# Moving the experts' down biases and the shared bias into one product per 128 tokens of the mixing stage

## The reference, cut to what matters

```python
x = x + attention(xn) + moe(xn)

# moe, over T = 4096 tokens, E = 8 experts, the best TOPK = 2 of them per token
scores = softmax(xt @ gate_w.T + gate_b)
top_w, top_i = top_k(scores, 2)
gate_dense = sum(one_hot(top_i, 8) * top_w[..., None], axis=1)        # (T, 8), two entries non-zero
def expert(w1e, b1e, w3e, b3e, w2e, b2e):
    h = silu(xt @ w1e.T + b1e) * (xt @ w3e.T + b3e)
    return h @ w2e.T + b2e                                            # b2e: the down bias
y = einsum('etd,te->td', outs, gate_dense)
z = silu(xt @ ws1.T + bs1) * (xt @ ws3.T + bs3) @ ws2.T + bs2         # bs2: the shared bias
moe = y + z
```

## Time and profile before

| what | value |
|---|---|
| time, median of 3 runs (lowest, highest) | 512.99 us (512.96, 513.41) |
| the profiled execution: its own time, its span | 512.58 us, 510.9 us |
| busy share of the span: PE, DVE, POOL, ACT | 88%, 75%, 52%, 46% |
| stages of the profiled execution, by PE | route to 97 us; experts 101 to 296.8; mixing 296.8 to 510.9 |
| TensorE clock granted, mean | 0.936 of full |
| DMA | 78.3 MB, 153 GB/s over the span |

### The profile page before, as it was taken

The page is one execution under the profiler, slowest core; times in us unless marked ns, Lnnn a source line. Parts: engine busy times, 40 slices in busy tenths (PEclk is TensorE's granted clock), DMA queues, the critical chain, the costliest instruction groups (busy, mean ns, idle before and its releaser), DMA issues.

```text
span 510.9 us, 8428 instructions
## 1 busy us (share of the span) xinstructions
PE 448.7 (88%) x2553; PEld 372.1 (73%) x2553; DVE 384.8 (75%) x704; ACT 232.8 (46%) x377; POOL 267.5 (52%) x227
## 2 busy tenths in 40 slices
PE   0768309489999999999999996999999999999997
PEld 0323105268988889888898974888888988898887
DVE  7677899535786777867775566999697969796964
ACT  1537335237668576685766563232323233233231
POOL 4402480374537548475482558886837464737200
PEclk9979755579999999999999998899999999999999
DMA  6999991134644443344444486252625252524111
GB/s 208 359 344 296 320 253 35 42 104 120 192 159 148 138 145 125 118 154 144 138 125 126 139 302 222 83 166 102 186 83 175 94 175 92 171 96 127 41 42 41
DMA packets 46662, 78.32 MB, mean 153 GB/s; under 512 B 6184, under 2 KB 32552, under 8 KB 46624
## 3 DMA queue, kind: packets, MB, share of 16 engines
q1 hardware_dynamic: 37808, 55.90, 31.6%
q0 software_dynamic: 8816, 21.93, 17.1%
HBM read 49.58 MB, written 28.21 MB: 152 GB/s over the span
## 4 chain that ended last, share of the span: by engine, by line
PE 68%; DVE 13%; DMA 7%; issue 7%; ACT 2%; POOL 1%; SPq 1%; DVEq 0%; POOLq 0%; ACTq 0%
PE ps_g L974 20%; PE ps_y L974 9%; PE ps_w L1389 5%; PE ps_w L1391 5%; PE ps_w L1390 5%; PE ps_x L968 3%; PE ps_h L992 3%; DMA xn_rows<-xn 3%; PE ps_w L1451 2%; PE ps_w L1453 2%; PE ps_w L1452 2%; PE ps_T L588 2%; DVE sa L1537 2%; PE ps_y L1001 2%; DVE part_a L1545 1%
## 5 line engine op out<-in xcount | busy, mean ns | idle before, releaser
L911 POOL DMA_INDIRECT xg<-xn_rows,tile_tok x71 | 69.9, 984 | 46.8 <-DVE tile_tok L783 18.8
L1359 POOL DMA_INDIRECT yg<-expert_rows,rows x64 | 70.0, 1093 | 23.9 <-issue 18.2
L1119 DVE TENSOR_TENSOR hid<-ps_g,act 128x512 f32<-128x512 f32 (+1 forms) x36 | 24.2, 672 | 48.7 <-ACT act L1043 48.3
L974 PE MATMUL ps_g<-w_hi,x_hi 128*128 x142 | 57.1, 402 | 0.4 <-issue 0.4
L974 PE MATMUL ps_g<-w_hi,x_lo 128*128 x142 | 56.8, 400 | 0.0
L974 PE MATMUL ps_g<-w_lo,x_hi 128*128 x142 | 56.5, 398 | 0.0
L1389 PE MATMUL ps_w<-col_hi,s_hi 128*128 128x512 f32 x128 | 50.7, 396 | 0.9 <-DVE res L1585 0.8
L1391 PE MATMUL ps_w<-col_hi,s_lo 128*128 128x512 f32 x128 | 50.2, 392 | 0.0
L1390 PE MATMUL ps_w<-col_lo,s_hi 128*128 128x512 f32 x128 | 50.2, 392 | 0.0
L1492 ACT ACTIVATE sact<-ps_w,vec_b 128x512 f32<-128x512 f32 x32 | 22.0, 688 | 58.7 <-PE ps_w L1391 58.7
L974 PE MATMUL ps_y<-w_hi,h_hi 128*128 x142 | 42.9, 302 | 0.5 <-DVE h_lo L1126 0.5
(11 more groups left out here) (210 smaller groups left out, 1292.8 us busy)
## 6 DMA issues: line engine op xcount, KB each, us to landing
expert_rows<-y SPq DMA_DIRECT2D x35, 256.0 KB, 2.2
table<-mix_tables SPq DMA_DIRECT2D x8, 768.0 KB, 7.5
xin<-x SPq DMA_DIRECT2D x16, 256.0 KB, 4.9
xn_rows<-xn SPq DMA_DIRECT2D x16, 256.0 KB, 5.7
xn_columns<-xT SPq DMA_DIRECT2D x8, 512.0 KB, 5.4
col<-xn_columns SPq DMA_DIRECT2D x8, 512.0 KB, 6.3
res<-x SPq DMA_DIRECT2D x16, 256.0 KB, 3.5
out<-res SPq DMA_DIRECT2D x16, 256.0 KB, 2.6
```

Source lines behind the costliest of these rows:

```text
L911: pool.indirect_dma_start(out=xg[b][:, t, :], out_offset=None, in_=xn_d[:, :], in_offset=bass.IndirectOffsetOnAxis(ap=tile_tok[:, 2 * a + ...
L974: mm = nc.tensor.matmul(out, x[:, k, :], w[:, ds(e, 1), k, cols].rearrange("p o n -> p (o n)"), start=(k == 0 and n == 0), stop=(last and ...
L1119: nc.vector.tensor_tensor(hid[:, 0:n, :], ps_g[a % 2][:, 0:n, FF:2 * FF], act1[:, 0:n, :], ALU.mult).then_inc(c_h, 1)
L1359: pool.indirect_dma_start(out=yg[a.buf(2)][:, k, q, :], out_offset=None, in_=y_d[:, :], in_offset=bass.IndirectOffsetOnAxis(ap=picked[a.bu ...
```

## The change

The down bias and the shared bias are no longer added where they arise. For each block of 512 tokens a 128 x 128 matrix `gT[:, i, :]` holds, for each of its four 128-token sub-tiles q, 32 rows (`TERMS`): the dense gates' high halves (8), their low rests (8), the high halves again (8), two rows of ones, and six of zeros. `rows_b[:, q, :]` holds beside them, in the partitions 32q to 32q+31, the down biases' high halves twice, their low halves, the shared bias's low and high half, and zero in all other partitions. One product of the two, 128 x 128 by 256 columns, opens each sub-tile's sum in `outputs`.

- In `route`, `ones2`, `bias_hl`, its zero fills, its split and its DMAs go. POOL makes the dense gates and their halves with five small operations behind its last indirect DMA, in `terms`.
- In `run_experts`, the 71 bias products go. Ahead of the first duo PE turns `terms` with 8 transposes into `ps_y`, ACT copies them to `gT` (2 copies). `b_all`, now 26 rows of b2 three times and bs2 twice, is loaded by 4 DMAs at duo 8 into `rows` (zeroed by POOL at duo 6); ACT makes the high halves at duo 14, POOL three operations at duo 16 that put high and low halves in place, by a mask from five tiny DVE operations at duo 8.
- In `mix`, POOL's `bias(a)` is replaced with `pick(a)`, a 128 x 128 copy of the step's `gT` into `g_now`, and four products are added per `outputs`. DVE's `experts(a, 0)` waits for the DMAs of `res` itself.

```diff
@@ route
-            nc.gpsimd.memset(pick2[:], 0.0).then_inc(s_two, 1)
-            pool.wait_ge(s_two, 1)
-            nc.gpsimd.memset(pick2[0:2, :], 1.0).then_inc(s_two, 1)
+            nc.gpsimd.memset(terms[:], 0.0).then_inc(s_terms, 1)
+            pool.wait_ge(s_terms, 1)
+            nc.gpsimd.memset(terms[:, :, 3 * E:3 * E + 2], 1.0).then_inc(s_terms, 1)
...
+            pool.wait_ge(s_mask, 3)
+            nc.gpsimd.tensor_tensor(dense[:], score, mask[:].rearrange("p e j -> p j e"), ALU.mult
+                                    ).then_inc(s_terms, 1)
+            pool.wait_ge(s_terms, 3)
+            nc.gpsimd.tensor_copy(dense_hi[:], dense[:]).then_inc(s_terms, 1)
+            pool.wait_ge(s_terms, 4)
+            nc.gpsimd.tensor_tensor(terms[:, :, E:2 * E], dense[:], dense_hi[:].bitcast(F32), ALU.subtract)
+            for n in (0, 2):
+                ins = nc.gpsimd.tensor_copy(terms[:, :, n * E:(n + 1) * E], dense_hi[:].bitcast(F32))
+            ins.then_inc(s_terms, 1)
...
-                nc.scalar.activation(bias_hl[:, a.i, :].bitcast(F32), ident[:, 0:1].broadcast_to([P, C]),
-                                     ACT.Copy, scale=0.0).then_inc(s_bzero, 1)
...
@@ run_experts
+                if a == A_ROWS:
+                    sp.wait_ge(c_zero, 1)
+                    for q in range(Q):
+                        sp.dma_start(rows[TERMS * q:TERMS * q + 3 * E + 2, q, :], b_all).then_inc(c_rows, 16)
...
+            def low_rows():
+                pool.wait_ge(c_rhi, 1)
+                pool.wait_ge(c_mask, 4)
+                nc.gpsimd.tensor_scalar(rows[:], rows[:], is_lo[:, 1:2], None, ALU.mult)
+                nc.gpsimd.tensor_scalar(rows_hi[:], rows_hi[:].bitcast(F32), is_lo[:, 2:3], None, ALU.mult
+                                        ).then_inc(c_own, 1)
+                pool.wait_ge(c_own, 1)
+                nc.gpsimd.tensor_tensor(rows_b[:], rows[:], rows_hi[:].bitcast(F32), ALU.add).then_inc(c_rowsb, 1)
...
             def down(a, es):
                 pe.wait_ge(c_hlo, a + 1)
+                if a < 2:
+                    pe.wait_ge(c_gT, a + 1)
                 at_least(pe, c_yc, a - 1)
                 for t in range(tiles(a)):
-                    three(ps_y[a % 2][:, t, :], h_hi[a % 2][:, t], h_lo[a % 2][:, t], es[t],
-                          slice(2 * FF, WALL), False)
-                    mm = nc.tensor.matmul(ps_y[a % 2][:, t, :], ones2[:],
-                                          bias_hl[:, ds(es[t], 1), :].rearrange("p o n -> p (o n)"),
-                                          start=False, stop=True)
+                    mm = three(ps_y[a % 2][:, t, :], h_hi[a % 2][:, t], h_lo[a % 2][:, t], es[t],
+                               slice(2 * FF, WALL), True)
                 mm.then_inc(c_y, 1)
...
-            pe.wait_ge(s_bias, 32)
+            pe.wait_ge(s_terms, 5)
+            for i in range(NSTEP):
+                mm = nc.tensor.transpose(ps_y[i // 4][:].rearrange("p t c -> p (t c)")[:, i % 4 * P:(i % 4 + 1) * P],
+                                         terms[:, i * Q:(i + 1) * Q, :].rearrange("p q n -> p (q n)"), ident[:])
...
@@ mix
-            def bias(a):
-                pool.wait_ge(b_res[a.buf(2)], (a.uses(2) + 1) * 32)
-                nc.gpsimd.tensor_tensor(res[a.buf(2)][:], res[a.buf(2)][:],
-                                        row_b2[:, None, :].broadcast_to([P, Q, C]), ALU.add).then_inc(b_xb, 1)
+            def pick(a):
+                at_least(pool, b_o, a.i * Q - Q)
+                nc.gpsimd.tensor_copy(g_now[a.buf(2)][:], gT[:, ds(a.i, 1), :].rearrange("p o n -> p (o n)")
+                                      ).then_inc(b_gc, 1)
...
                 def mixed(q):
+                    nc.tensor.matmul(ps_w[q][:, 0:C], g_now[a.buf(2)][:], rows_b[:, q, :],
+                                     start=True, stop=False)
                     for k in range(KC):
                         three_rows(ps_w[q][:, 0:C], a_hi, a_lo, k, slice(q * P, (q + 1) * P), o_hi, o_lo,
-                                   k == 0, False)
+                                   False, False)
...
                 if g == 0:
-                    dve.wait_ge(b_xb, a.i + 1)
+                    dve.wait_ge(b_res[buf], (a.uses(2) + 1) * 32)
                     dve.wait_ge(b_gath[buf], (a.uses(2) + 1) * 16 * TOPK * Q)
```

More of the change, by code:

```diff
@@ L54 @@
 EPS = 1e-5
+TERMS = 32
 PIECE = 256
@@ L218, in _, with route @@
                 mix_vector(dve)
-def route(nc, kept, x, first, decay, vec_tf, vec_td, gate_w, gate_b, w_all, w_first, nw_d, b_all, xn_d, xT_d, ident, slots, gates,
-          tile_tok, tile_exp, w_hi, w_lo, bias_hl, ones2):
+def route(nc, kept, x, first, decay, vec_tf, vec_td, gate_w, gate_b, w_all, w_first, nw_d, xn_d, xT_d, ident, slots, gates,
+          tile_tok, tile_exp, w_hi, w_lo, terms):
     with ExitStack() as ctx:
@@ L801, in sem @@
             return kept.enter_context(nc.semaphore(name))
-        s_tok, s_xout, s_bias = placed
+        s_tok, s_xout, s_terms = placed
         raw_vr, col0 = vr[0], col[0]
+        rows, rows_hi, gT, rows_b = bias
+        row32 = sb("row32", [P, 1], I32)
+        is_lo = sb("is_lo", [P, 3], F32)
         NG = 4
@@ L947, in gpsimd @@
                     gather(a + AHEAD)
+                if a == A_ZERO:
+                    nc.gpsimd.memset(rows[:], 0.0).then_inc(c_zero, 1)
+                    nc.gpsimd.iota(row32[:], pattern=[[0, 1]], base=0, channel_multiplier=1).then_inc(c_iota, 1)
+                if a == A_LO:
+                    low_rows()
                 if r == 1 and v == NPIECE:
@@ L1078, in scalar @@
             act.wait_ge(s_tok, 1)
+            for h in range(2):
+                act.wait_ge(c_turn, h + 1)
+                nc.scalar.activation(gT[:, 4 * h:4 * h + 4, :].rearrange("p j n -> p (j n)"),
+                                     ps_y[h][:].rearrange("p t c -> p (t c)"), ACT.Copy).then_inc(c_gT, 1)
             halves(0)
@@ L1094, in scalar @@
                     halves(v)
+                if a == A_HI:
+                    act.wait_ge(c_rows, 16 * Q)
+                    act.wait_ge(c_zero, 1)
+                    nc.scalar.activation(rows_hi[:], rows[:], ACT.Copy).then_inc(c_rhi, 1)
                 if a == DUOS - 4:
@@ L1240, in mix @@
         sa = sb("sa", [P, KC * B, TIMES + 1], F32)
+        g_now = [sb(f"g_now{b}", [P, P], F32R) for b in range(2)]
         table = [sb(f"table{b}", [P, 3, KC, TIMES], F32) for b in range(2)]
```

95 lines of the change are left out of this document (50 added, 45 removed).

## The result

| | before | after |
|---|---|---|
| time, median (lowest, highest; runs) | 512.98 us (512.75, 513.41; 4) | 504.82 us (503.35, 506.79; 4) |
| profiled execution: time, span | 512.58, 510.9 us | 504.14, 502.3 us |
| TensorE clock granted, mean | 0.936 | 0.939 |

By the medians the kernel is faster by 8.2 us. The ratio of the runs is 0.9851, which is 7.6 us, with a 95% interval of 0.983 to 0.9873 (6.5 to 8.7 us). The prediction said 504.3 us and a range of 501.0 to 508.5. The runs of after spread more (3.4 us) than those of before (0.7 us).

What follows compares the result with a forecast made beforehand. PE was taken to bound the expert and mixing stages. The terms, -8.2 + 3.8 - 2.9 - 2.8 + 1.6 - 0.2 = -8.7 us, led from the median of 512.99 to 504.3 us, range 501.0 to 508.5.

Steps and rivals of the forecast that it cites:

- Removed products: Expert stage: 71 bias products go at 0.12 us each, three of them giving nothing; -8.2 us.
- POOL gets 6 us more ... behind 193 us of PE, 0: Expert stage: POOL's added memset, scalings and addition fit beside 80 us free and cost 0.
- Added products: Mixing stage, bound by PE: 32 products at 0.12 us each at the full clock; +3.8 us.
- The stall ahead of values(1): PE's 4.57 us idle shrinks to some 2.5, the clock probably kept; -2.9 us (bounds -1.2 and -3.5).
- The late starts: Mixing steps: most of PE's six late starts, waiting for DVE, end; -2.8 us (bounds -1.7 and -3.1).
- POOL's five in the route: Route: POOL's five new operations block DVE's one-hot chain and delay tile_tok; +1.6 us (bounds 0 and 5.0).
- The start: Start: ACT's zero fills, DVE's split of the biases and one DMA go; -0.2 us (0 to -0.5).
- duos 5.11 us apart: Sign in the expert stage: the distance of two duos' up falls from 5.36 us to 5.12.
- the clock kept at 0.23: Sign behind values(1)'s idle time: first products 0.24 us apart if the clock is kept, 0.43 if fallen.
- `tile_tok` 1.1 us later: Sign in the route: tile_tok comes 1 to 2 us later than at 94.83.
- DVE rows of 1.49 and 2.59 us: Sign in the route: DVE rows of 1 us and more between 77 and 81 us.
- the idle time of 2 to 3 us: Sign ahead of values(1): PE's idle time there is 2 to 3 us.

Runs made afterwards that it cites:

- e1: The kernel before with its 71 down bias products left out and nothing else changed; 510.36 us, ratio 0.9845.
- e3: The kernel after with its 32 added products in the mixing stage left out; 507.32 us, ratio 0.9785.
- e11: The kernel after with the terms' five POOL operations on VectorE and ScalarE and the two low-row scalings on ScalarE; 505.49 us, ratio 0.9813.
- e2: The kernel before without POOL's eight additions of the shared bias, DVE waiting for the residual rows' DMAs itself; 512.27 us, ratio 0.9883.
- e4: The kernel before with the five POOL operations on the dense gates added to route, their result unused; 520.27 us, ratio 1.0047.
- e5: The kernel after with the route's five POOL operations written on VectorE and ScalarE instead; 510.59 us, ratio 0.9865.
- e8: The kernel after with the terms' five operations on VectorE and ScalarE, two scalings on ScalarE, 14 unused transposes added; 508.77 us, ratio 0.9821.
- e10: The kernel after with terms' five operations on VectorE and ScalarE, scalings on ScalarE, 14 unused transposes, on another chip; 504.31 us, ratio 0.9798.

## Why the prediction was right, step by step

**Removed products, -8.2 us: right in size, and the stage kept 7.0 of it.** e1 measured 8.0. In after the stage gave 7.0, since 1.1 us came back in the one wait at 226 us.

**The step that failed: "POOL gets 6 us more ... behind 193 us of PE, 0".** Both halves were wrong. The scalings take 2.88 and 2.86 us, not 1.3 each. They were priced from the 0.645 us for 512 elements, an operation whose two numbers stand in the instruction; these read a number per partition. And a free third of an engine is no cover when the work comes in one piece. Behind the 8.2 us POOL's queue had no idle time of over 0.31 us until 231 us, so its `den` was ready only at 223.34. DVE waited 2.87 us for it, where before the same wait was 1.15 us. DVE's two reciprocals of `den` stand in its queue ahead of `hid` and `h_lo`, so these came at 225.06 and 225.60, and PE, whose next transposes need them, waited 0.77 us. The DMA that ACT waited for (2.07 us at 220.45) is late by the same work, but that wait is not the one that held PE: ACT had its `act` ready at 222.61, and `hid` began 2.4 us later. Stage shares cannot show this; the chain of the tables had to be followed.

**Added products, +3.8 us: right, as closely as the runs tell.** e3 gives 3.4 to 4.0, give or take 2; by its trace 2.8 to 3.3, and some 0.6 more without its one wait for `res`.

**The stall ahead of values(1), -2.9 us (bounds -1.2 and -3.5): the mechanism right, the size short.** Up to `outputs(0)` after gained 4.3 us (2.9 and 1.4 in the table), beyond the bound. The copy has its 0.3 us, the clock was kept, `s_lo` became the next wait (0.52 us), all as written. The miss is the idle time, 1.58 us for 2.5: POOL's work there came 0.9 us sooner behind `values(0)` (15.9 us, 307.87 less 291.98) than before (16.8 us, 313.57 less 296.80); the prediction had left all ahead of the addition as it was. It begins with POOL's copy of the slots ahead of the gathers, which ended 1.8 us sooner behind `values(0)` in after; the gathers then took 0.9 us longer. The copy meets a long operation of DVE. Here are both in before, in after and in e11:

```profile
298.58 2.29 DVE L1641 TENSOR_TENSOR s_lo<-raw_s,s_hi 128x2048 fp32r<-128x2048 f32 x1 [2.19 <-ACT s_hi L1521]
299.60 1.32 POOL L1354 COPY rows<-slots 128x8 int32<-128x8 int32 x1 [2.86 <-DMA expert_rows<-y]
```

```profile
294.10 0.19 POOL L1398 COPY rows<-slots 128x8 int32<-128x8 int32 x1 [2.17 <-DMA expert_rows<-y]
294.15 2.29 DVE L1690 TENSOR_TENSOR s_lo<-raw_s,s_hi 128x2048 fp32r<-128x2048 f32 x1 [2.66 <-ACT s_hi L1570]
```

```profile
294.46 2.29 DVE L1696 TENSOR_TENSOR s_lo<-raw_s,s_hi 128x2048 fp32r<-128x2048 f32 x1 [2.64 <-ACT s_hi L1576]
294.60 2.21 POOL L1404 COPY rows<-slots 128x8 int32<-128x8 int32 x1 [2.33 <-DMA expert_rows<-y]
```

Where DVE came first, POOL's copy lasted until DVE's operation ended (300.92 against 300.87 in before, 296.81 against 296.75 in e11). In after POOL came first, by 0.05 us, and its copy took 0.19. Of the nine traces with after's mixing stage POOL came first in seven, with 1.17 to 1.58 us idle ahead of `values(1)` and the clock kept. DVE came first in e3 and e11, with 2.79 us idle and the clock lost, and there the stretch to `values(1)` took 19.8 us where the others have 18.1 to 18.6. So 1.2 us of this gain hang on a lead of 0.02 to 0.05 us; that the profiled run of after had it is luck.

**The late starts, -2.8 us: right.** From `outputs(0)` to the end the kernel lost 0.5 us with 3.8 us of products added, so 3.3 us of waits went. e2 shows that DVE's part sufficed. Not all of POOL's grip on DVE is gone: the timeline of DVE in a step of after has a copy of four numbers that lasts as long as POOL's low half beside it (POOL's row second).

```profile
396.66 2.26 DVE L1600 COPY sa<-sa 128x4 f32<-128x4 f32 x1
```

```profile
395.79 3.09 POOL L1411 TENSOR_TENSOR col_lo<-col,col_hi 128x1024 fp32r<-128x1024 f32 x1 [9.85 <-ACT col_hi L1523]
```

PE does not wait for it there.

**POOL's five in the route, +1.6 us (bounds 0 and 5.0): in the bounds, rather low.** The pair of kernels shows +2.3, e4 alone 2.4 as a time. The length of the operations was mis-sized: in after the five take 4.7 us (some of it their own waiting beside DVE), where the half of larger ones gave 2.2. DVE lost less than their length because it works on between them. The five traces of kernels with after's route all have 34.0 or 34.1 us; those without the operations on POOL have 31.7 to 33.0, so the price is 1.0 to 2.4, and moving them (e5, e8, e10, e11: 31.8 to 32.5) gives most of it back. The rule that the prediction took from the Trainium skill, "SBUF — State Buffer", section "SBUF: two separate sides", is the right side of that choice: by it a block was certain, without it the term might have been 0, and the trace agrees, with 2.59 us for `hot_in`.

**The start, -0.2 us (0 to -0.5): too small.** The route's first 61 us became 1.3 us shorter. Whether that is the split, the fills or the DMA was not tried.

**The first products, not in the sum: +1.0 us**, of which traces of unchanged starts show 0.7 too (e1, e4), so it is not shown to be a term of the change.

Of the signs given to look for: duos 5.11 us apart (5.12 said), the clock kept at 0.23, `tile_tok` 1.1 us later, DVE rows of 1.49 and 2.59 us came; the idle time of 2 to 3 us was 1.58, and one row of PE is still marked with `s_lo`, in `outputs(0)`. The misses are -1.4 and -0.5 in the mixing stage, -1.1 at the start, +1.2 in the experts, +0.7 in the route and +1.1 up to and in the first products; their sum is 0.0. The terms' directions and causes were right but for POOL's in the expert stage; that the total came so much closer than its terms is luck.

## What to carry to other kernels

A correction that is linear in the rows is cheapest where rows are already summed, even if it costs products there: the 32 products (3.8 us) cost less than the 71, and the gain beside them came from taking a 2.35 us operation out of the queue that held up another engine. Price small work on a second engine by the place and not by its share: ask what it blocks (a port of the neighbour) and which chain passes through that queue behind it (here the wait came 16 us after the work had ended); put such work where that engine's own wait is long, or on an engine that shares no port. And where every term is a microsecond or two, compare variants on one chip: single edits that their traces showed at work could not be seen in ratios from different ones.
